# The last attention written as a stage of its own: values with V stationary, q and y made transposed, P scaled by its sum on GpSimd, normalization by batch

## The reference, cut to what matters

```python
def _L1_attn_b_ref(x, W_lat, b_lat, W_d, b_d, W_proj, b_proj):
    NH, L = (16, 128)
    k = x @ W_lat + b_lat                                   # B, T, 128
    q = (x @ W_d + b_d).reshape(Bx, Tx, NH, L)
    q = jnp.transpose(q, (0, 2, 1, 3))
    att = jnp.einsum('bhtl,bsl->bhts', q, k) * (1.0 / math.sqrt(L))
    att = jnp.where(causal[None, None], att, -jnp.inf)
    att = jax.nn.softmax(att, axis=-1)
    y = jnp.einsum('bhts,bsl->bhtl', att, k)
    y = jnp.transpose(y, (0, 2, 1, 3)).reshape(Bx, Tx, NH * L)
    return y @ W_proj + b_proj
...
    x = x + _L1_attn_b_ref(_layernorm(x, axis=-1), ...)
```

## Time and profile before

| | us |
|---|---|
| median of 3 runs | 4331.57 (4328.63 to 4335.73) |
| the profiled execution's own time | 4335.42 |
| its span, first to last instruction | 4333.7 |
| TensorE busy in the span | 3392.9 (78%) |
| VectorE | 2820.9 (65%) |
| ScalarE | 2204.1 (51%) |
| GpSimd | 1801.8 (42%) |

### The profile page before, as it was taken

How to read it: one execution, slowest core, us unless ns; L and a number is a source line. 1 busy time by engine, 2 the same in 40 slices (tenths; PEclk the granted TensorE clock), 3 DMA queues, 4 the chain that set the end, 5 groups by cost and what they waited for, 6 DMA issues and landing times. The chain is left out here.

```text
span 4333.7 us, 73351 instructions
## 1 busy us (share of the span) xinstructions
PE 3392.9 (78%) x20792; PEld 2702.4 (62%) x20795; DVE 2820.9 (65%) x6113; ACT 2204.1 (51%) x5817; POOL 1801.8 (42%) x3108
## 2 busy tenths in 40 slices
PE   7799938908887396199999999997373999999374
PEld 3355636706775375188788787786352888888253
DVE  5699856646776665578588687685533656666442
ACT  3699703406775043288588687784022444444111
POOL 0399814477561255455265364452273000000165
PEclk9799958959999598599999999999575999999566
DMA  2011133530001245300000000001434000000524
GB/s 81 23 49 49 37 137 98 134 91 1 1 1 71 76 133 121 99 16 20 9 20 19 10 20 16 12 20 61 122 63 117 1 2 1 2 2 1 172 47 102
DMA packets 133309, 222.79 MB, mean 51 GB/s; under 512 B 28624, under 2 KB 106448, under 8 KB 131104
## 3 DMA queue, kind: packets, MB, share of 16 engines
q1 hardware_dynamic: 99184, 148.95, 10.3%
q0 software_dynamic: 33792, 69.83, 7.4%
HBM read 163.71 MB, written 54.80 MB: 50 GB/s over the span
## 5 line engine op out<-in xcount | busy, mean ns | idle before, releaser
L1256 POOL DMA_INDIRECT ex_xr<-scratch_rows,mo_token x288 | 286.0, 993 | 347.7 <-issue 313.3
L598 POOL TENSOR_TENSOR sc_h<-sc_h,sc_c 128x512 f32<-128x512 f32 x256 | 326.9, 1290 | 198.7 <-DVE sc_h L635 190.6
L3240 DVE TENSOR_TENSOR sa_pT<-bank,sa_pT 128x512 fp32r<-128x512 f32 x512 | 329.9, 686 | 34.1 <-ACT sa_pT L3108 30.3
L3100 ACT ACTIVATE sa_p<-bank,sa_nm 128x512 f32<-128x512 f32 x512 | 346.7, 689 | 2.5 <-DVE sa_nm L3231 2.5
L635 DVE TENSOR_TENSOR_SCAN sc_h<-sc_da,bank 128x512 f32<-128x512 f32 x256 | 311.1, 1220 | 38.5 <-ACT sc_da L578 23.7
L2929 PE MATMUL bank<-sa_kT,sa_qT 128*128 128x512 f32 x1024 | 333.1, 436 | 1.5 <-DVE residual L3207 1.5
L3227 DVE TENSOR_REDUCE sa_mx<-bank 128x2 f32<-128x1024 f32 x256 | 312.2, 1220 | 26.1 <-PE bank L2931 22.0
L1322 PE MATMUL bank<-mo_w_gu,ex_xT 128*128 (+2 forms) x1152 | 314.5, 401 | 2.4 <-issue 1.0
L2953 PE MATMUL bank<-sa_pT,sa_v 128*128 128x256 f32 x2048 | 301.4, 290 | 16.7 <-DVE sa_pT L3240 16.4
L1370 ACT ACTIVATE ex_xT<-bank 128x256 f32<-128x256 f32 (+1 forms) x288 | 105.1, 365 | 404.9 <-PE bank L1304 378.8
L1170 POOL IOTA rg_m<- 128x48 f32 x2 | 0.3, 171 | 702.2 <-POOLq L1654 674.8
(11 more groups left out here) (389 smaller groups left out, 9652.3 us busy)
## 6 DMA issues: line engine op xcount, KB each, us to landing
scratch_ys<-ex_yo SPq DMA_DIRECT2D x192, 128.0 KB
mo_w_gu<-in_w_gu SPq DMA_DIRECT2D x2, 9216.0 KB, 25.6
sc_c<-scratch_c SPq DMA_DIRECT2D x64, 256.0 KB, 3.1
sa_share<-scratch_shares SPq DMA_DIRECT2D x256, 64.0 KB, 2.6
mo_w_dn<-in_w_dn SPq DMA_DIRECT2D x2, 4608.0 KB, 47.3
mo_w_dn<-in_w_dn SPq DMA_DIRECT2D x2, 4096.0 KB, 33.6
scratch_rows<-ln_stage POOLq DMA_DIRECT2D x64, 128.0 KB, 5.6
ex_xr<-scratch_rows,mo_token POOLq DMA_INDIRECT x288
```

Of the source, the lines that this page charges most:

```text
L598: pool.tensor_tensor(h, h, C[u], ALU.mult).then_inc(used.sem, 1)
L1256: pool.indirect_dma_start(xr[u][:, :], None, rows, bass.IndirectOffsetOnAxis(ap=token[:, i:i + 1], axis=0), bounds_check=rows.shape[0] - 1 ...
L3100: act.activation(pr[h][:, :], SC[2 * s_ + h][:, :], ACT.Exp, bias=nm[:, col:col + 1], scale=SCALE, accum_out=rs[:, col:col + 1]).then_inc( ...
L3240: dve.tensor_tensor(spot(1), PT[h][:, :].rearrange("p (k n) -> p k n", k=TPB), spot(0).bitcast(F32), ALU.subtract).then_inc(*inc("kept_d"))
```

## The change

`attention(c, a)` and its use for this layer are replaced by `latent(c)`, written for this layer alone. All loops are written out, with no register arithmetic.

- Normalization: the statistics of all 16 tiles come first as before, but a batch is normalized, turned, split and projected to keys by itself (`stand`, `turn_x`, `keep_x`, `low_x`); batches 1 to 3 during heads 7 to 11 of the batch before.
- Keys come out transposed, all 512 tokens in one bank (`project_k`); they take their bias as a per-partition number. They are turned once for V (`turn_k`). Both are split, and kT carries the scale 1/sqrt(128), so that the maximum needs no scaling.
- q of a head comes out transposed, 512 tokens in one bank (`project_q`); no turning. The bias is a per-partition number for ScalarE's high part and VectorE's low part.
- The head is the outer loop and the query tile the inner one. A step N has the scores of unit N, the turning of P of N-3, one piece of the values of a head two back and one of four pieces of the output product of the head three back. Behind every fourth step comes the projection of the head two ahead.
- P is multiplied by 1/sum on GpSimd before it is turned, so that y needs no normalization; the reciprocal is VectorE's. All turned P are split, high on ScalarE and low on VectorE.
- Values have V as the stationary operand, split in two like the turned P, and give y transposed: for key block kb, `TRIPLE` over the query tiles kb to 3. y is split and goes into the output product with no turning. The product of all 16 heads is summed in two banks (`OUT`), which are cleared by a matmul with zeros.
- Loads: wq comes in two halves; wo takes its place in SBUF when its halves have been split, and is split in units 4 to 6.
- x, k, v and q all pass through one bank, `QB`, in the order of the list `USES`.
- In `rotary`, GpSimd makes three tiles of a group, then `add_parts`, then the fourth tile.

```diff
@@ GpSimd
+                for N in range(NU):
+                    cut = slice(0, keys(N % TPB))
+                    pool.wait_ge(*at("own_n", N + 1))
+                    pool.tensor_scalar(pr[N % 4][:, cut], pr[N % 4][:, cut], rinv[:, N % 8:N % 8 + 1], None, ALU.mult) \
+                        .then_inc(*inc("normed"))
@@ TensorE
-                        for kb in range(nb):
-                            heads = a.HG if a.KH == a.H else 1
...
-                            last = pe.matmul(OB[qt % 2][:, hh * P:(hh + 1) * P],
-                                             pT[u % 2][:, kb * P:(kb + 1) * P], v,
-                                             start=(kb == 0), stop=(kb == nb - 1))
+                    for kb in blocks:
+                        for p_, v_ in TRIPLE:
+                            last = pe.matmul(OB[:, kb * P:SEQ], vv[b % 2][v_][:, kb * P:(kb + 1) * P],
+                                             pT[M % 2][p_][:, kb * SEQ + kb * P:(kb + 1) * SEQ],
+                                             start=(kb == 0 and p_ + v_ == 0),
+                                             stop=(kb == TPB - 1 and (p_, v_) == TRIPLE[-1]))
...
+                for N in range(NU + 12):
+                    M, qt = divmod(N, TPB)
+                    b, h = divmod(M, H)
+                    V, piece = divmod(N - 8, TPB)
+                    Y, part = divmod(N - 12, TPB)
+                    if N < NU:
+                        score(N)
+                    if 3 <= N < NU + 3:
+                        turn_p(N - 3)
+                    if 0 <= V < NH and piece < 3:
+                        values(V, ((0,), (1,), (2, 3))[piece])
+                    if 0 <= Y < NH:
+                        product(Y, part)
+                    if qt == 1 and 8 <= h < 10 and b + 1 < BATCH:
+                        turn_x(b + 1, h - 8)
...
+                    if qt == 3 and M + 2 < NH:
+                        project_q(M + 2)
@@ ScalarE
+                    if 3 <= N < NU + 3:
+                        high_p(N - 3)
+                    if N < NU:
+                        expo(N)
...
+                    if N >= 10 and (N - 10) % TPB == 0 and (N - 10) // TPB < NH:
+                        keep_y((N - 10) // TPB)
...
+                    if qt == 3 and M + 2 < NH:
+                        keep_q(M + 2)
@@ VectorE
+                    if N < NU:
+                        maximum(N)
+                    if 1 <= N < NU + 1:
+                        invert(N - 1)
+                    if 3 <= N < NU + 3:
+                        low_p(N - 3)
...
+                    if N >= 10 and (N - 10) % TPB == 0 and (N - 10) // TPB < NH:
+                        low_y((N - 10) // TPB)
+                    if N >= H * TPB + 9 and (N - 9) % (H * TPB) < TPB:
+                        add_out((N - 9) // (H * TPB) - 1, (N - 9) % (H * TPB))
+                    if h == 7 and b + 1 < BATCH:
+                        stand(b + 1, qt)
...
+                    if qt == 3 and M + 2 < NH:
+                        low_q(M + 2)
@@ rotary, GpSimd
                     if I + 2 < NG:
-                        put_group(I + 2, range(TPB))
+                        put_group(I + 2, range(TPB - 1))
                     if I >= 1:
                         add_parts(I - 1)
+                    if I + 2 < NG:
+                        put_group(I + 2, (TPB - 1,))
```

More of the change, by code:

```diff
@@ L1676, in _ @@
[L1676 to L1694 removed]
+                pool.affine_select(out=mask[:, :], in_=mask[:, :], compare_op=ALU.is_ge, fill=NEG,
+                                   base=0, pattern=[[-1, P]], channel_multiplier=1).then_inc(*inc("made"))
@@ new lines, in project_k @@
+                def project_k(b):
+                    wait_bank(pe, "k", b, 0)
+                    pe.wait_ge(*at("xlow", 2 * (b + 1)))
+                    if b == 0:
+                        pe.wait_ge(*at("wlow", 1))
+                    for k in range(KC):
+                        for x_, w_ in TRIPLE:
+                            last = pe.matmul(QB[:, :], WK[w_][:, k * D:(k + 1) * D],
+                                             xb[b % 2][x_][:, k * SEQ:(k + 1) * SEQ], start=(k == 0 and x_ + w_ == 0),
+                                             stop=(k == KC - 1 and (x_, w_) == TRIPLE[-1]))
+                    last.then_inc(*inc("kvp"))
@@ new lines, in score @@
+                def score(N):
+                    M, qt = divmod(N, TPB)
+                    b = M // H
+                    if qt == 0:
+                        pe.wait_ge(*at("qlow", M + 1))
+                        if M % H == 0:
+                            pe.wait_ge(*at("klow", b + 1))
+                    if N >= 2:
+                        pe.wait_ge(*at("exped", N - 1))
+                    bank = SC[N % 2]
+                    for i, (q_, k_) in enumerate(TRIPLE):
+                        pe.matmul(bank[:, 0:keys(qt)], qT[M % 3][q_][:, qt * P:(qt + 1) * P], kT[b % 2][k_][:, 0:keys(qt)],
+                                  start=(i == 0), stop=False)
+                    pe.matmul(bank[:, qt * P:keys(qt)], identb[:, :], mask[:, :], start=False, stop=True) \
+                      .then_inc(*inc("scored"))
@@ L2165, in attention @@
[L2165 to L2177 removed]
+                st = Steps(dve, sig["own"])
@@ new lines, in _, with stand @@
+                st.then(dve.reciprocal(rstd[:, :], tmp[:, :]))
+                def stand(b, i):
+                    n = b * TPB + i
+                    if b and i == 0:
+                        dve.wait_ge(*at("xturned", 2 * b))
+                    dve.tensor_scalar(stage[:, i * D_MODEL:(i + 1) * D_MODEL], c.x[:, n * D_MODEL:(n + 1) * D_MODEL],
+                                      mean[:, n:n + 1], rstd[:, n:n + 1], ALU.subtract, ALU.mult) \
+                       .then_inc(*inc("stood"))
```

836 lines of the change are left out of this document (295 added, 541 removed).

## The result

The changed kernel takes 4213.29 us (median of 4 runs, 4211.57 to 4214.08) against 4331.32 us before: ratio 0.973, interval 0.9709 to 0.9743, 118 us less.

What follows compares the result with a forecast made beforehand. TensorE was taken to bound the last attention stage; terms (a) to (f) sum to 595.4 us against 696.8 (-101.4), and rotary's -2.5 makes -104 in total: 4228 us for the median, range 4206 to 4280.

Steps and rivals of the forecast that it cites:

- (a): Start of the last attention stage: first score 33.4 us after the first statistics instead of 49.3.
- (b): The last attention's 64 heads at 8.40 us each, less two projections already done: 534.6 us; floor 8.2 a head.
- rival C: Last attention: everything hides, 8.2 us a head and half of (d) and (e): -20, 4208 us; chance 0.06 below 4208.
- (c): Last attention: x, k and v of three batches inside the stream, 2.8 us each, 8.4 us.
- (e): Last attention's batch changes: eight additions on VectorE and k's two copies holding up a maximum, 2 us each, 6 us.
- (d): Filling of the last attention's pipeline: about 17.5 us at half clock for 9.5 of work, 8 us.
- (f): End of the last attention stage: last P, y and additions one behind another, 5 us.
- The GpSimd step: Last attention: GpSimd multiplies P by the reciprocal before turning; wide P 1.3 us in a 2.0 us window, wait costed at nothing.
- Rival A: Last attention: the order of three engines binds, +28 to +91 us; chance 0.20 between 4248 and 4290, 0.08 beyond.
- Rival B: Last attention: GpSimd becomes the bound and the change is slower, 4426 us at 9 ns a column; chance 0.04.
- Rival D: Last attention's values: stationary V saves nothing, +15, 4243 us; sign: 512-column matmuls over 0.26 apart; chance inside the sum's 0.62.
- Rotary: Rotary stage: y's parts added before the fourth tile, addition 1.2 us earlier at three of four batches; -2.5 us.

Runs made afterwards that it cites:

- values_blocks: Changed kernel with V still stationary but the values' moving operands cut into blocks of 128 columns, 28 matmuls a head instead of 12: 4281.4 us, ratio 0.9883.
- turn_split_early: Changed kernel with the turnings of P in two pieces around the scores and the wide sum's reciprocal moved forward on VectorE: 4207.3 us, ratio 0.9712.
- start_and_wo: Changed kernel with x split first, a bank each for first k, v and two queries, and output weights split in eight pieces: 4199.7 us, ratio 0.9694.
- start_first: Changed kernel with x split ahead of the query weights and a bank each for the first k, v and two queries: 4205.3 us, ratio 0.9698.

## Why the prediction was right, and where not

**What bounds: right, with less margin than stated.** The wait for GpSimd was given a cover of 0.4 to 1.3 us a head; it is 0.26. TensorE sets the head: 99.8% busy, a head 1.2 us longer where it gets more (`values_blocks`). VectorE has 0.67 x 8.02 = 5.4 us a head and ScalarE 5.1, under the 6.0 and 5.8 taken.

**Start (a): right.** 33.4 us, as forecast. It was also the part with the most left in it.

**The heads (b): the term that was mis-sized.** Forecast 8.40 us with a floor of 8.2, measured 8.02, 64 x 0.38 = 24 us, the whole miss. By pieces, forecast to measured: scores 2.20 to 1.89, masks 0.24 to 0.27, turnings 0.76 to 0.81, values 2.20 to 2.10, product 1.52 to 1.57, projection 1.48 to 1.39. The step that failed is "three score matmuls: 0.37 us at 128 columns, 0.44 at 256, 0.78 at 512" together with "P turned 0.76": in the earlier trace rows each score group stands behind a turning and carries 0.08 us of it, and I gave these 0.08 to the scores and, by using the score groups as the price of the values, to the values again. That is four times 0.08, or 0.31 of the 0.38; `turn_split_early` shows that this time exists once. Most of the rest is the projection, 0.09 shorter. The floor of 8.2, which rival C rests on, was too high for the same reason.

**The smaller terms.** (c) and (e), 14.4 forecast: in each of three batches heads 8 to 11 take 8.47, 8.47, 9.41 and 8.89 and the fourth of the next batch 8.79, together 3.9 over five heads, 11.8 in all. (d) and (f), 13 forecast: what is left, 572.4 - 33.4 - (64 x 8.02 - 2.8) - 11.8 = 16.7. The filling was dearer: the output weights' subtractions of 2.28 us stand ahead of two maxima, at 3369.23 and 3372.56, and with these weights in smaller pieces the longest head of the filling takes 8.94 us (`start_and_wo`) instead of 12.13 (`start_first`).

**The GpSimd step: right in the path, low in the price.** Its order came true, and it was laid out up to 0.4 us late (the turning at 3.87 us of the head instead of 4.1, the fourth exponential's end at 8.2 instead of 8.6, the reciprocal's at 10.0 instead of 10.4), and the window for the wide P, from the reciprocal to the turning, is 1.93 us (3531.76 to 3533.69) where 2.0 was forecast. I took 1.3 us; it is 1566 ns, inside the bounds and near the upper one (1.64). By the Trainium skill, GPSIMD Engine Reference, section "Engine selection", an operation with one input runs at roughly line rate there; the prediction's estimate from that was near 0.65 us. The trace disagrees (groups by form, mean ns of one):

```profile
L1614 POOL TENSOR_SCALAR la_p<-la_p,la_rinv 128x512 f32<-128x512 f32 x64 | 100.2, 1566 | 72.2 <-DVE la_rinv L1898 72.2
L1614 POOL TENSOR_SCALAR la_p<-la_p,la_rinv 128x384 f32<-128x384 f32 x64 | 79.6, 1244 | 121.6 <-DVE la_rinv L1898 121.6
...
L1614 POOL TENSOR_SCALAR la_p<-la_p,la_rinv 128x128 f32<-128x128 f32 x64 | 38.7, 605 | 35.8 <-DVE la_rinv L1898 35.8
```

"Beyond it each 0.1 us costs 6.4" was right: 1.57 us more on the path, 1.31 beyond the cover, made the stage 81.8 us longer (76 by the medians) where that rule says 1.31 x 64 = 84.

**Rival A** (the order of three engines binds) did not come true, but missed by 0.26 us a head; its price, TensorE at 0.95, came from no row; the length of the ring would have given one. **Rival B** (GpSimd's sum) is refuted twice: 4.3 us a head, and 1.5 us more of it are free off the ring. **Rival C** (everything hides) came nearest in the number, 4208, but not by its own way: a head is below its 8.2, and instead of half of (d) and (e) going, (c) and (e) are 2.6 less and (d) and (f) 3.7 more. **Rival D** (V stationary saves nothing) falls with the changed kernel's own rows: the values of a head take 2.10 us instead of 2.43, and those of 512 columns stand 0.23 us apart, under its sign of 0.26. `values_blocks` shows on what that hangs: at 0.116 a block of 128 columns a head is 1.2 us longer.

**Rotary:** forecast -2.5 for the run. The shortened waits came true (3.4 us); that the stage was 5.6 us ahead at one moment and 1.9 at its end goes with the clock, which at its end is not the same in every execution of the same code. What is left of it in the run is not shown.

Together: the stage was forecast 23.0 us too long (24.1 for the heads and 2.6 for (c) and (e) too much, 3.7 for filling and end too little). Rotary's 2.5 us do not show between these two profiles, and some 4 us of the 124.4 were the late clock in the profile of before. That leaves 16.5; the medians show 15. That the total came out this near owes something to luck: the surpluses and shortfalls partly cancel, and the run-to-run spread ahead of the stage is as large.

## What to carry to other kernels

Beside the sum of each engine, look for rings: follow what releases what until you are back at the same step one period later, and compare each ring's length, not only the longest, with the period of the busiest engine. The same 1.5 us of GpSimd work cost some 80 us on the ring and nothing beside it, and a cut of 1.4 us on TensorE was worth 20 us because the ring stood 0.26 us below. When a group is priced by the distance from start to start, price its neighbour in the same stretch, and in the order in which they will stand: time booked on the follower is otherwise counted twice.

## What the runs showed of the hardware beyond that

- A multiplication by a per-partition number on GpSimd, fp32 on 128 partitions, costs 605, 924, 1244 and 1566 ns at 128, 256, 384 and 512 columns: 0.29 us and 2.5 ns a column. With a constant instead of the number from memory 512 columns took 1.49 us.
- The clock of the same code is not the same in every execution. At the rotary stage's last products seven of thirteen profiles with the same code there have the lower level (634 or 635 ns for 256 columns) and six the higher (379), and it costs them some 2.7 us (8.6 instead of 6.0 from the first to the last product). At the two ends before it, where the waits are 1.1 us shorter than in the kernel before, all thirteen have 1.00 where that had 0.89. No run here shows what decides it.
- Two profiles of an identical stage can differ by 4 us with the moment at which the clock rises (granted clock 0.50 against 0.95 in 3366 to 3374), and the start of the last attention by 17 us over thirteen profiles with the same code ahead of it. Differences of that size should be read stage by stage, with the clock beside them.
